# Probability sums two steps behind the scores, and A products ahead of state products, in a two-layer attention and time-mixing kernel

## The reference, cut to what matters

```python
# layer 0: x is (2, 1024, 256); 16 query heads in 8 groups of 2, head size 16
q, k = rope(x @ W_Q.T), rope(x @ W_K.T)
v = x @ W_V.T
scores = einsum('bsdkg,btdk->bkgst', q, k) / sqrt(256)
w = softmax(scores, axis=-1)
ctx = einsum('bkgst,btdk->bkgsd', w, v)
s = ctx @ W_O.T                       # times silu of a feed-forward net, added to x

# layer 1: time mixing, 4 heads of 64, then routed experts as the gate
def step(state, (k_t, v_t, w_t, r_t)):
    state = (1 - w_t)[:, None] * state + k_t[:, None] * v_t[None, :]
    y_t = r_t @ state
out = y @ Wout
```

## Time and profile before

| | |
|---|---|
| Time, median of three runs | 901.56 us |
| The profiled execution's own time | 912.6 us |
| Its span | 910.8 us |
| TensorE busy | 821.9 us (90%) |
| VectorE busy | 687.6 us (76%) |
| ScalarE busy | 521.1 us (57%) |
| GpSimd busy | 358.5 us (39%) |

### The profile page before, as it was taken

One profiled execution on the slowest core, in us unless ns is written; L12 is line 12 of the kernel. 1 busy time (PEld: TensorE's weight loads), 2 busy tenths in 40 slices (PEclk: granted clock), 3 DMA queues, 4 the chain that ended last, 5 costly groups with the idle time before them and its releaser, 6 DMA issues. The chain is left out here.

```text
span 910.8 us, 18081 instructions
## 1 busy us (share of the span) xinstructions
PE 821.9 (90%) x6672; PEld 529.5 (58%) x6672; DVE 687.6 (76%) x1023; ACT 521.1 (57%) x955; POOL 358.5 (39%) x294
## 2 busy tenths in 40 slices
PE   3999999999999999989999999997669898999995
PEld 3854333333333333333487887986657477999884
DVE  5789999999999999991267655669996456555477
ACT  4420787787778777877743324444674334666442
POOL 5430454347534753467013000005874670344300
PEclk9975999999999999999999999998785779999997
DMA  6595122222222222000085000001014222344352
GB/s 227 208 231 214 34 51 53 52 51 51 49 51 49 50 50 50 16 15 15 13 254 58 1 1 12 2 1 56 4 53 196 77 83 46 111 121 125 103 169 71
DMA packets 59511, 69.97 MB, mean 77 GB/s; under 512 B 24768, under 2 KB 46400, under 8 KB 59040
## 3 DMA queue, kind: packets, MB, share of 16 engines
q1 hardware_dynamic: 55272, 58.28, 24.4%
q0 software_dynamic: 3408, 9.38, 2.9%
q10 hardware_dynamic: 744, 1.15, 0.4%
HBM read 40.06 MB, written 26.62 MB: 73 GB/s over the span
## 5 line engine op out<-in xcount | busy, mean ns | idle before, releaser
L671 ACT ACTIVATE probs_t<-psum 128x512 f32<-128x512 f32 x512 | 271.8, 601 | 108.0 <-PE psum L771 105.5
L685 DVE TENSOR_REDUCE row_max<-psum 128x1 f32<-128x1024 f32 x256 | 298.9, 1216 | 14.2 <-PE psum L755 14.0
L612 POOL TENSOR_TENSOR lut_sum<-lut_sum,lut_tmp 128x1072 f32<-128x1072 f32 x60 | 151.0, 2517 | 169.0 <-DVE lut_tmp L710 168.3
L755 PE MATMUL psum<-KS,QS 48*128 48x512 f32 x512 | 185.4, 466 | 15.4 <-DVE row_max L685 15.0
L771 PE MATMUL psum<-QS,KS 50*128 50x512 f32 x512 | 197.5, 460 | 1.0 <-ACT probs_t L671 1.0
L771 PEld LDWEIGHTS psum<-QS,KS 50*128 50x128 f32 x512 | 83.4, 186 | 138.0 <-ACT probs_t L671 134.1
L783 PE MATMUL psum<-probs_t,VS 128*32 128x512 f32 x1024 | 141.3, 611 | 8.2 <-ACT o_sb L553 8.2
L755 PEld LDWEIGHTS psum<-KS,QS 48*128 48x128 f32 x512 | 81.4, 197 | 68.5 <-DVE row_max L685 60.9
L2267 POOL DMA_INDIRECT y_rows<-y_slot,ids x39 | 37.4, 959 | 70.9 <-ACT y_slot L2326 70.6
L710 DVE TENSOR_SCALAR lut_tmp<-lut_idx,lut 128x1072 f32<-128x1072 int32 x60 | 48.3, 807 | 10.1 <-POOL lut_sum L612 10.1
L783 PEld LDWEIGHTS psum<-probs_t,VS 128*32 128x32 f32 x1024 | 23.8, 108 | 45.3 <-ACT probs_t L671 37.9
(11 more groups left out here) (300 smaller groups left out, 1833.6 us busy)
## 6 DMA issues: line engine op xcount, KB each, us to landing
KS<-k_rows SPq DMA_DIRECT2D x31, 192.0 KB, 4.6
QS<-q_rows SPq DMA_DIRECT2D x31, 192.0 KB, 5.0
x_rows<-zero_rows SPq DMA_DIRECT2D x1, 4992.0 KB, 18.2
x_slot<-x_rows SPq DMA_DIRECT2D x39, 128.0 KB
m_raw<-experts_w SPq DMA_DIRECT2D x2, 2432.0 KB, 12.2
q_rows<-part SPq DMA_DIRECT2D x8, 512.0 KB, 8.8
y_token<-y_rows SPq DMA_DIRECT2D x8, 512.0 KB, 7.6
x_tok<-x SPq DMA_DIRECT2D x4, 512.0 KB, 7.6
```

The lines of the kernel that those rows point to most:

```text
L612: nc.gpsimd.tensor_tensor(wsum[:, c % 2, :], wsum[:, c % 2, :], wtmp[:, slot % 2, :], ALU.add).then_inc(lut_add, 1)
L671: nc.scalar.activation(pt[:, k % NPT, :], ring(k)[:], ACT.Exp, scale=float(E) ** -0.5).then_inc(p_ready, 1)
L685: nc.vector.tensor_reduce(mx[:, n % 2, col:col + 1], m.psum[:, 2 * (k % 2):2 * (k % 2) + 2, :], AX_XY, ALU.max).then_inc(max_done, 1)
L755: mm = nc.tensor.matmul(MX[k % 2][h][:], QS[n % NQK][rows(g, NROW), st * P:(st + 1) * P], KS[n % NQK][rows(g, NROW), h * BLK:(h + 1) * BLK ...
```

## The change

- `weigh` is called two steps behind the scores (LAG = 2) instead of one: in step (n, t) the products of step t - 2, in the first two steps of an n those of the last two of the n before. After the last step two calls of `weigh` follow instead of one.
- There are ten probability tiles instead of eight.
- `take_o` stands before exponential i = 7 instead of i = 4.
- In the steps that have no maxima left, the four scores come in the order (2, 0, 3, 1): the heads alternate. In the others the order is as before.
- The longer `probs_t` reaches into memory that the feed-forward net's tiles have; `f_h` and `f_silu` change places, `f_silu` begins behind the probability tiles, and VectorE's first product into `f_h` waits until all products of `weigh` are done.
- `output(g)`: first all 16 A products of the group, then the waits for the states and the receptance, then all 14 state products. The first A product of each bank starts the accumulation, and the last state product of each bank ends it.

```diff
--- before.py
+++ after.py
@@ -459,8 +459,10 @@
     b = m.p0
     QS, KS, qk_in, load_qk = m.QS, m.KS, m.qk_in, m.load_qk
     wtmp = at("lut_tmp", [P, 2, m.PIECE], F32, b); b += 2 * m.PIECE * 4
-    NPT = 2 * NJ
+    LAG = 2
+    NPT = LAG * NJ + 2
     pt = at("probs_t", [P, NPT, BLK], F32, b); b += NPT * BLK * 4
+    m.probs_end = b
     b = m.p0 + 34304
     osb = at("o_sb", [P, 2, BLK], F32, b); b += 2 * BLK * 4
     m.ctxT = at("ctxT", [P, KC, T], F32, b); b += KC * T * 4
@@ -498,7 +500,10 @@
     NEARLY = 2
     m.NEARLY = NEARLY
     AHEAD = 10
-    PAIRED = (2, 3, 0, 1)
+    def paired(n, t):
+
+        return (2, 3, 0, 1) if (n + 1) * NST + AHEAD + G * t < NG * NST else (2, 0, 3, 1)
+
     MX = [bank[0:2], bank[2:4]]
     SP = bank[4:7]
     OB = bank[7]
@@ -661,7 +666,7 @@
                     take_high(act, n // 4 - 1)
             for i in range(NTT * NJ):
                 k = n * NTT * NJ + i
-                if i == 4 and n >= 1:
+                if i == LAG * NJ - 1 and n >= 1:
                     take_o(act, n - 1)
                 act.wait_ge(s_ps, k + 1)
                 if k >= NPT:
@@ -759,7 +764,7 @@
 
         def scores(n, t, i):
             k = (n * NTT + t) * NJ + i
-            g, half = divmod(PAIRED[i], NJ // G)
+            g, half = divmod(paired(n, t)[i], NJ // G)
             if t == 0 and i == 0:
                 pe.wait_ge(m_in, 16 * G * (n + 1))
             if n == 0 and t == 0 and i == 0:
@@ -776,7 +781,7 @@
             bb, kv = divmod(n, KV)
             for i in range(NJ):
                 k = (n * NTT + t) * NJ + i
-                j = PAIRED[i]
+                j = paired(n, t)[i]
                 pe.wait_ge(p_ready, k + 1)
                 if t == 0 and i == 0 and n >= 1:
                     pe.wait_ge(o_done, n)
@@ -816,10 +821,10 @@
                     maximum(k, h)
                 scores(n, t, 0)
                 scores(n, t, 1)
-                if t >= 1:
-                    weigh(n, t - 1)
+                if t >= LAG:
+                    weigh(n, t - LAG)
                 elif n >= 1:
-                    weigh(n - 1, NTT - 1)
+                    weigh(n - 1, NTT - LAG + t)
                 scores(n, t, 2)
                 scores(n, t, 3)
                 for h in range(2):
@@ -827,7 +832,8 @@
                 early = n * NTT + t - (NG * NTT - 6 * NEARLY)
                 if early >= 0:
                     up_two(early)
-        weigh(NG - 1, NTT - 1)
+        for t in range(NTT - LAG, NTT):
+            weigh(NG - 1, t)
 
     m.attend_sync, m.attend_gpsimd, m.attend_scalar, m.attend_vector, m.attend_tensor = (
         attend_sync, attend_gpsimd, attend_scalar, attend_vector, attend_tensor)
@@ -850,8 +856,9 @@
     m.rstd1 = at("rstd1", [P, NT], F32, b); b += NT * 4
     m.p3 = b
     hh = at("f_hh", [P, 3, BLK], F32R, b); b += 3 * BLK * 4
+    hf = at("f_h", [P, 2, BLK], F32, b); b += 2 * BLK * 4
+    b = max(b, m.probs_end)
     sg = at("f_silu", [P, 2, BLK], F32, b); b += 2 * BLK * 4
-    hf = at("f_h", [P, 2, BLK], F32, b); b += 2 * BLK * 4
     m.xb = at("x_norm2", [P, NT, E], F32, m.after_ctx - KC * T * 4)
     assert b <= m.after_ctx - KC * T * 4
     zero = at("zero_rows", [P, E], F32, b); b += E * 4
@@ -1005,6 +1012,9 @@
         for tb in range(NB):
             for c, (i0, n) in enumerate(pieces):
                 k = tb * NI + c
+                if k == 0:
+
+                    dve.wait_ge(m.pv_done, m.PV_ALL)
                 if k == 2:
                     m.invert(dve, m.NG - 1)
                 dve.wait_ge(silu_done, k + 1)
@@ -2085,9 +2095,7 @@
 
         def output(g):
             bb, ct = divmod(g, KC)
-            pe.wait_ge(st_done, (g + 1) * (NC - 1))
             pe.wait_ge(ad_put, 4 * (g + 1))
-            pe.wait_ge(r_done, (NL - 1) * NCH + g + 1)
             if g >= 2:
                 pe.wait_ge(tyl_done, g - 1)
             def out(c, h):
@@ -2095,12 +2103,16 @@
 
             for c in range(NC):
                 for h in range(NH):
-                    mm = nc.tensor.matmul(out(c, h), m.V[:, bb * NC + c, ct * P + h * LD:ct * P + (h + 1) * LD],
-                                          A[g][:, h * NC + c, :], start=True, stop=(c == 0))
-                for h in range(NH if c else 0):
+                    nc.tensor.matmul(out(c, h), m.V[:, bb * NC + c, ct * P + h * LD:ct * P + (h + 1) * LD],
+                                     A[g][:, h * NC + c, :], start=(c % 4 == 0), stop=False)
+
+            pe.wait_ge(st_done, (g + 1) * (NC - 1))
+            pe.wait_ge(r_done, (NL - 1) * NCH + g + 1)
+            for c in range(1, NC):
+                for h in range(NH):
                     ch = slice(h * LD, (h + 1) * LD)
                     mm = nc.tensor.matmul(out(c, h), ST[g % 2][ch, c, :], group(m.R, g)[ch, c * CH:(c + 1) * CH],
-                                          start=False, stop=True)
+                                          start=False, stop=(c % 4 == 3))
             mm.then_inc(ty_ps, 1)
 
         def out_product(i):
```

## The result

The changed kernel takes 891.91 us (median of 885.5, 890.14, 893.68, 897.51) against 902.62 for the kernel before in the same company (901.4, 901.56, 903.67, 909.23). The ratio is 0.985, 95% interval 0.981 to 0.989: 13.7 us. I had said 25.9. Twice more beside the kernel before, on two other chips, it gave 0.982 (0.979 to 0.985) and 0.983 (0.979 to 0.987). So the gain is 14 to 16 us wherever it was measured, a little over half of the forecast. A few runs of some kernels fell in a slower state of the chip, at a lower granted clock, and the ratios leave them out.

What follows compares the result with a forecast made beforehand. VectorE bounds attention until maxima end, then TensorE; TensorE's outputs limit time mixing, with VectorE next. Savings of 6.5 + 4.5 + 15 = 26 us take the median from 901.56 to 876 us; range 864 to 892.

Steps and rivals of the forecast that it cites:

- Once-per-n wait: Attention with maxima: VectorE's 0.62 us wait per n for a TensorE product mostly goes, saving 6.5 us.
- the case in which VectorE's buffers take up the rest: Attention with maxima: VectorE's two buffers absorb what remains of the wait at each n boundary, saving 7.7 us.
- Last stretch: Attention without maxima: alternating heads shorten 12 steps from 2.98 to 2.61 us, saving 4.5 us.
- Outputs: Time mixing: grouping products by kind and filling output 0's wait save 15 us, after 6 off for possible stalls.
- With the wait filled I take full clock: Time mixing outputs: A products fill the 2.23 us wait, so TensorE is taken at full clock, 3.6 us per output.
- Savings: Time mixing outputs: the filled wait plus each output's profiled time less 3.6 us, 20.9 us in all.
- over to the median unscaled: Whole kernel: differences worked out in the 912.6 us profile apply unchanged to the 901.56 us median.
- A: Rival: TensorE stays at half clock through time mixing's outputs, only attention's 11 us and 5 come; 886 us, chance 0.14.
- B: Rival: in attention TensorE's ring loop replaces VectorE's wait, so the 6.5 us don't come; 882 us, chance 0.10.
- D: Rival: in time mixing's outputs a group in a run still costs 0.37 us, weight loads unhidden; 883 us, chance 0.02.
- C: Rival: half clock lasts past the outputs through output projections and first shared block; slower, 905.5 us, chance 0.05.
- the routed tiles would be caught by the scattered rows: After time mixing: routed tiles need the last scattered row, so a gain above some 20 us would be caught there.

Runs made afterwards that it cites:

- e3: The changed kernel, unchanged, run beside its parts on the first chip; ratio to the kernel before 0.982 (0.979 to 0.985), 16.0 us faster.
- e2: The kernel before with only the new output step, attention as before; ratio to the kernel before 0.996 (0.994 to 0.998), 3.6 us faster.
- e10: The changed kernel with eight buffers for routed rows instead of six, on the third chip; ratio to the kernel before 0.984 (0.981 to 0.988).
- e6: The kernel before with only the heads alternating in steps without maxima; ratio to the kernel before 0.998 (0.995 to 1.001), 2 us.
- e1: The kernel before with all attention edits and the old output step; ratio to the kernel before 0.991 (0.988 to 0.994), 8.0 us faster.
- e5: The kernel before with only sums two steps behind, ten probability tiles and the later copy; 908.9 and 909.2 us in two usable runs, no ratio.
- e4: The changed kernel with VectorE's routed rows behind the low parts of the weights and the last low_y; ratio to the kernel before 0.988.

## Why the prediction was half right

*Once-per-n wait, 6.5 us.* Right. Over the 13 full intervals the copies span 399.7 - 113.0 = 286.7 us before and 393.9 - 115.4 = 278.5 after: 8.2 us, a little over the 7.7 that I gave as the case in which VectorE's buffers take up the rest.

*Last stretch, 4.5 us.* Right in the step, 2.61, and a little less in the sum. From TensorE's first early feed-forward product to VectorE's first product into `f_h` it is 32.6 us in e3, the new form at full clock, instead of 36.2 in the profile of before: 3.6 us. Part of the rest is that only 11 distances lie between 12 steps.

*What attention then lost.* Not foreseen, and some 3 us: TensorE at half clock. Windows 390 to 430 us of e2 (sums one step behind) and e10 (two):

```profile
390.00:430.00 40.00, 37.11 (x200) 13.27 (x196) 22.19 (x25) 29.95 (x57) 32.27 (x15) 1.00 0.08 16
```

```profile
390.00:430.00 40.00, 37.65 (x168) 12.07 (x164) 16.59 (x18) 25.36 (x48) 29.64 (x14) 0.74 0.06 13
```

Of four profiles with the old lag, this window has a clock of 1.00 in three and 0.96 in one. Of the eight full-attention profiles with the new lag and the late copy it has 0.74 to 0.96 in seven; the eighth (e3) has its spell at 220 to 250 us. By the intervals between copies the spell costs 1.5 to 8 us (against an undisturbed interval of 22.4 there, e3's) and 2.4 in e3, 4.7 in the mean, and 0 to 2.7, 1.3 in the mean, in the four (against 22.7, e6's). TensorE's longest wait for maxima there is 1.7 us in the new order and 1.05 in the old, and in e1 the clock falls right behind it: the wait ends at 395.90, and the granted clock is 0.69 in the next 4 us and 0.50 from 404 to 408. But e3 has the same wait of 1.70 us, up to 399.0, and its clock stays at 1.00 there. That the wait is the cause was not tried, and e3 shows that it is not enough. The last copy of attention starts at 437.8 to 445.6 us (mean 440.9) in those eight, against 446.9 to 448.5 in three with the old attention: 7 us, as e1's 8.0 says.

*Outputs, 15 us.* This step failed, in its size. Of the mechanism, the runs of one kind were right: 3.6 us an output, 0.22 a group, and output 0's wait filled. "With the wait filled I take full clock" came out as a number, but not for the reason given: e1 has the full clock with the wait unfilled. And "Savings: 2.2 + (9.0 - 3.6) + (6.7 - 3.6) + (12.05 - 3.6) + (5.4 - 3.6) = 20.9" took each output's time as the old form's own. The old form takes 5.36 (e1); the rest was the stall and half clock of that execution, as e5 and e6 have them too. I had seen that in output 2 only, left it there with 6 us, and then carried the profile's difference "over to the median unscaled", though the median holds none of it. By rows that stood there: the one undisturbed output is 5.44, so 2.2 + 4 x (5.44 - 3.6) = 9.6 at the most. Of these, TensorE's new waits for the state of chunk 3 and for the last `low_y` take 2.9 + 2.2 = 5.1 back in the changed kernel, since VectorE stands behind the scatter, and 4.5 is left. In e2 they are longer (waits, 675 to 770 us):

```profile
PE psum L445 <- DVE ty_l L1941: 3.7, 1, 3.7
PE psum L2104 <- DVE state L2001: 2.7, 1, 2.7
```

With e1's figures for the old form, 2.7 + 4 x (5.36 - 3.6) - 6.4 leaves 3.3, and e2 measured 3.6. The prediction had no term for these waits. With attention's 11 the sum is 15.5 and the median 886; with what attention gave and lost in the profiles, 8.2 + 3.6 - 3.4 + 4.5, it is 12.9 us, beside the 13.7 to 16.0 measured.

*The rivals.* A (half clock through the outputs), B (the ring loop takes over, 6.5 lost) and D (0.37 a group in runs) are shown wrong by the rows after, C too. The remark that the routed tiles would be caught by the scattered rows was right in kind and wrong in place: it set in from the first few us, through VectorE's wait for a buffer and, in e4, ScalarE's.

The measured 888 (0.985 of 901.56) lies in the range up to 892, near where A had put it and for another reason. That is luck in part: the high end was built from A and B, and neither came about.

## What to carry to other kernels

When the profiled execution is slower than the median of the runs, find where the excess lies before working out a saving: look for repeats of the same work with different times, and take the shortest as the cost. A saving worked out inside the excess is not in the median, or both versions pay the excess, as here on the second and third chip. And where a chain in order on one engine (VectorE here) feeds three others, moving work together on a fourth soon meets that chain's next wait.

## What the runs showed of the hardware

- TensorE can stand for "issue" between single products, 0.2 to 1.7 us at a time, over 4 to 20 us, in the stage in which GpSimd scatters. It came in that stage in all eight profiles of two chips and in none of four on a third.
- The same kernel (before) has medians of 903.8, 914.6 and 917.9 us on three chips, yet the ratio of after to before agrees to 0.001 between the two that ran both.
- In e1 the time goes with the mean granted clock: its six runs lie from 892.95 us at 0.938 to 899.86 at 0.927. In e3 it does not: 889.04 us at 0.939, 888.38 at 0.934.
- A wait of TensorE of about the same length can stand before a half clock or before a full one: 2.23 us and then 0.50 (profile of before, output 0), 2.68 us and then 1.00 (e1, output 0).
